# Self-attention scores through one folded weight product

## The reference, cut to what matters

```python
x = x + cross_attention(layernorm(x), ctx)      # 16 heads of 32, context of 257
n = layernorm(x)                                # self-attention, one head of 512
q = n @ Wq + bq;  k = n @ Wk + bk;  v = n @ Wv + bv
scores = einsum('btd,bsd->bts', q, k) / sqrt(512)
scores = where(causal, scores, -1e30)
m = max(scores, axis=(-2, -1));  e = exp(scores - m)
w = e / sum(e, axis=(-2, -1))                   # one sum for a whole 32 x 32 matrix
x = x + einsum('bts,bsd->btd', w, v)
x = x + ffn(layernorm(x))                       # 512 -> 2048 -> 512, signs of the weights
```

## Time and profile before

| | |
|---|---|
| Median of 3 executions | 2920.38 us (2919.47 to 2922.21) |
| Span of the profiled execution | 2917.1 us |
| Median less span | 3.3 us |
| PE busy | 2794.1 us, 96% |
| DVE, ACT, POOL busy | 57%, 43%, 27% |
| Stages in the profile | queries to 126 us, cross-attention to 1918, round 0 to 1997, rounds 1 to 15 and the tail to 2917 |

### The profile page before, as it was taken

How to read it: one execution, slowest core, us unless ns; L and a number is a source line. 1 busy time by engine, 2 the same in 40 slices (tenths; PEclk the granted TensorE clock), 3 DMA queues, 4 the chain that set the end, 5 groups by cost and what they waited for, 6 DMA issues and landing times. The chain is left out here.

```text
span 2917.1 us, 54809 instructions
## 1 busy us (share of the span) xinstructions
PE 2794.1 (96%) x18492; PEld 1704.0 (58%) x18492; DVE 1668.3 (57%) x3620; ACT 1267.4 (43%) x2954; POOL 776.4 (27%) x1530
## 2 busy tenths in 40 slices
PE   7999999999999999999999999957999999899999
PEld 4455555555555555555555555534666666566666
DVE  7555555555555555555555555556665666656664
ACT  4344444444444444444444444423433443344444
POOL 2233333333333333333333333211111111111110
PEclk9999999999999999999999999978999999999999
DMA  4211111111111111111111111022000000000000
GB/s 143 83 56 55 62 41 40 40 48 41 40 40 48 41 40 40 48 41 40 40 48 41 40 40 48 13 84 66 15 30 15 15 14 22 22 14 14 14 23 15
DMA packets 65959, 118.49 MB, mean 41 GB/s; under 512 B 12016, under 2 KB 32496, under 8 KB 65392
## 3 DMA queue, kind: packets, MB, share of 16 engines
q1 hardware_dynamic: 65904, 117.76, 12.4%
HBM read 109.06 MB, written 8.65 MB: 40 GB/s over the span
## 5 line engine op out<-in xcount | busy, mean ns | idle before, releaser
L656 DVE SCALAR_TENSOR_TENSOR kT_lo<-psum,kT_hi 128x512 f16<-128x512 f32 x256 | 177.1, 692 | 440.2 <-ACT kT_hi L587 440.2
L591 ACT ACTIVATE v_hi<-psum 128x512 f16<-128x512 f32 x256 | 152.8, 597 | 552.7 <-PE psum L746 552.7
L746 PE MATMUL psum<-c_hi,xWk_hi 128*128 128x512 f16 x1024 | 388.1, 379 | 2.3 <-PEq L136 2.3
L746 PE MATMUL psum<-xWv_hi,c_hi 128*128 128x512 f16 x1024 | 388.3, 379 | 0.0
L746 PE MATMUL psum<-xWv_lo,c_hi 128*128 128x512 f16 x1024 | 388.1, 379 | 0.0
L746 PE MATMUL psum<-xWv_hi,c_lo 128*128 128x512 f16 x1024 | 388.1, 379 | 0.0
L746 PE MATMUL psum<-c_lo,xWk_hi 128*128 128x512 f16 x1024 | 388.1, 379 | 0.0
L746 PE MATMUL psum<-c_hi,xWk_lo 128*128 128x512 f16 x1024 | 388.1, 379 | 0.0
L118 POOL TENSOR_TENSOR c_lo<-ctx_raw,c_hi 128x1024 f16<-128x1024 f32 x128 | 272.5, 2129 | 429.8 <-ACT c_hi L583 419.2
L662 DVE SCALAR_TENSOR_TENSOR v_lo<-psum,v_hi 128x512 f16<-128x512 f32 x256 | 177.1, 692 | 360.4 <-ACT v_hi L591 360.4
L597 ACT ACTIVATE e<-psum,neg_max 128x257 f32<-128x257 f32 x512 | 236.3, 474 | 281.9 <-DVE neg_max L651 281.9
(11 more groups left out here) (195 smaller groups left out, 5986.9 us busy)
## 6 DMA issues: line engine op xcount, KB each, us to landing
ctx_raw<-in_ctx_main SPq DMA_DIRECT2D x128, 512.0 KB, 3.3
xs<-in_x SPq DMA_DIRECT2D x8, 1024.0 KB, 5.5
v_rep<-v_last_rows SPq DMA_DIRECT2D x512, 16.0 KB, 2.3
xb<-in_x SPq DMA_DIRECT2D x16, 512.0 KB, 3.3
out<-res_out SPq DMA_DIRECT2D x32, 256.0 KB, 2.0
ffn_raw<-in_w_t SPq DMA_DIRECT2D x11, 512.0 KB, 3.4
late_raw<-in_late_w SPq DMA_DIRECT2D x4, 1024.0 KB, 4.7
res<-in_w_t SPq DMA_DIRECT2D x5, 512.0 KB, 3.5
```

The lines of the kernel that those rows point to most:

```text
L591: nc.scalar.mul(v_hi[u][:, t, :], v_bank(t), W_UNSCALE).then_inc(v_hi_done, 1)
L656: nc.vector.scalar_tensor_tensor(out=kT_lo[r][:, m, :, 0:S], in0=k_bank(m), scalar=W_UNSCALE, in1=kT_hi[r][:, m, :, 0:S], op0=ALU.mult, op ...
L746: mm = nc.tensor.matmul(bank, a, b, start=(n == 0), stop=(n == len(steps) - 1))
```

## The change

Since `q k^T = (n Wq + bq)(n Wk + bk)^T`, the scores can be written as `(n F + c) n^T + (n u + d)`, where `F = Wq Wk^T`, `c = Wk bq`, `u = Wq bk` and `d = bq . bk`. The term `n u + d` is one number for each query token, added to its whole row of scores.

In `cross_queries` SP loads bq, bk, Wk and Wq. At the last token group PE transposes both weights (8 times `turn`, 4 float32 transposes each), two ahead of each quarter of the group's projections; then `fold` forms F (48 matmuls of 512 columns), u repeated on all partitions (12 of 512), c (48 of one column) and d (12 of one column). ACT and DVE split the turned weights into the slots of Wo and Wv, which cross-attention fills later, and F into its own. ACT converts the first contexts after the last projection. Two late weights, not four, are loaded in `cross_attention`. In `token_stages` there are two parts r of 24 matmuls, not four, and the scores multiply their result by the transposed tokens themselves. DVE gets `row_biases`: two multiply-and-sum instructions over 128x512 and two additions to the mask. Two DMAs of bias columns at the start of the stage go.

```diff
@@ cross_queries, SP
+            sp.dma_start(bias[:, 0:KC], bq).then_inc(bias_landed, 16)
+            sp.dma_start(bias[:, KC:], bk).then_inc(bias_landed, 16)
+            for u in range(2):
+                load(2 + u, u)
+            load_folded(3)                    # waits for w_lo_done >= 2
+            load_folded(4)                    # waits for w_lo_done >= 3
-            with sp.Fori(1, NG // 2) as i:
+            with sp.Fori(2, NG // 2) as i:
...
@@ cross_queries, PE, last group
                 if not more:
                     last_tokens()
+                    for m in range(KC):
+                        turn(2 * m)
+                        turn(2 * m + 1)
+                        queries(g, u, [m])
+                    fold()
+                    return
+            def turn(j):
...
+                for c in range(KC):
+                    mm = nc.tensor.transpose(psum[:, TURN_BANK[j % 4], c * P:(c + 1) * P],
+                                             raw[1 - j // KC][:, c, k * P:(k + 1) * P], ident[:, :])
+            def fold():
+                pe.wait_ge(turn_lo_done, 2 * KC)
+                for m in range(KC):
+                    accumulate(psum[:, TURN_BANK[m], :],
+                               [(a[:, k, m * P:(m + 1) * P], b[:, k, :]) for k in range(KC)
+                                for a, b in passes(*wqT, *wkT)]).then_inc(fold_ps, 1)
+                pe.wait_ge(rep_done, 2)
+                pe.wait_ge(q_lo_done, NG * KC)
+                accumulate(u_bank, [(a[:, k, :], b[:, k, :]) for k in range(KC)
+                                    for a, b in passes(bk_rep_hi, bk_rep_lo, *wqT)]).then_inc(u_ps, 1)
+                for m in range(KC):
+                    accumulate(c_bank[:, m:m + 1],
+                               [(a[:, k, m * P:(m + 1) * P], b[:, k:k + 1]) for k in range(KC)
+                                for a, b in passes(*wkT, bias_hi, bias_lo)])
+                accumulate(dot_bank, [(a[:, k, :], b[:, k:k + 1]) for k in range(KC)
+                                      for a, b in passes(bk_rep_hi, bk_rep_lo, bias_hi, bias_lo)]
+                           ).then_inc(c_ps, 1)
@@ cross_queries, ACT, last group
                     last_tokens()
+                    for m in range(KC):
+                        high_turned(2 * m)
+                        high_turned(2 * m + 1)
+                        high_q(g, [m])
+                    first_contexts()
+                    for m in range(KC):
+                        high_folded(m)
+                    ...                       # u_row, c_col, bias_dot out of PSUM
@@ token_stages, PE
-                    for r in range(4):
-                        hi, lo = late["sWq" if r < 2 else "sWk"]
+                    for r in range(2):
+                        hi, lo = late["folded"]
...
-                    pe.wait_ge(s["qk_lo_done"], 4 * (n + 1))
+                    pe.wait_ge(s["qk_lo_done"], 2 * (n + 1))
...
-                                                    for q, k in passes(qk_hi, qk_lo, qk_hi, qk_lo)])
+                                                    for q, k in passes(qk_hi, qk_lo, x2T_hi, x2T_lo)])
@@ token_stages, DVE, between the split of x2T and F(5)
+            def row_biases(n):
+                for t in range(T):
+                    dve.wait_ge(s["norm2_done"], T * n + t + 1)
+                    nc.vector.tensor_tensor_reduce(
+                        out=products[:, t, :], in0=xn[:, t, :], in1=u_row[:, :], scale=1.0,
+                        scalar=bias_dot[:, :], op0=ALU.mult, op1=ALU.add,
+                        accum_out=row_bias[:, t:t + 1]).then_inc(s["row_bias_done"], 1)
+                for t in range(T):
+                    dve.wait_ge(s["row_bias_done"], T * n + t + 1)
+                    past(dve, s["sc_done"], BPT * n)
+                    nc.vector.tensor_scalar(row_mask[:, t, :], mask[:, :], row_bias[:, t:t + 1], None,
+                                            ALU.add).then_inc(s["row_mask_done"], 1)
@@ token_stages, SP
-            for dst, src in ((bqk_col[:, 0:KC], bq), (bqk_col[:, KC:], bk), (b1_col[:, :], b1)):
-                sp.dma_start(dst, src).then_inc(s["consts_landed"], 16)
+            sp.dma_start(b1_col[:, :], b1).then_inc(s["consts_landed"], 16)
```

More of the change, by code:

```diff
@@ L21 @@
 FEATURES = 512
+FOLD_SCALE = 16.0
+WO, FOLDED, SWV = range(3)
 def past(engine, semaphore, count):
@@ L56, in perceiver_block @@
     KC = D // P
-    LATE = late_w.shape[0]
+    LATE = 3
     with ExitStack() as whole:
@@ L185, in cross_queries, with turned @@
         v_last_bank = psum[:, 1, :]
+        TURN_BANK = (2, 3, 0, 1)
+        wqT = (late_hi[:, WO], late_lo[:, WO])
+        wkT = (late_hi[:, SWV], late_lo[:, SWV])
+        u_bank = psum[:, 4, :]
+        c_bank = psum[:, 5, 0:KC]
+        dot_bank = psum[:, 5, KC:KC + 1]
+        def turned(j):
+            return (wqT if j < KC else wkT), j % KC
         def t_bank(t):
@@ L291, in low_q, with low_turned @@
                         op1=ALU.subtract).then_inc(q_lo_done, 1)
-            def one(g, u, more=True):
+            def low_turned(j):
+                dve.wait_ge(turn_hi_done, j + 1)
+                (hi, lo), k = turned(j)
+                nc.vector.scalar_tensor_tensor(out=lo[:, k, :], in0=psum[:, TURN_BANK[j % 4], :],
+                                               scalar=W_SCALE, in1=hi[:, k, :], op0=ALU.mult,
+                                               op1=ALU.subtract).then_inc(turn_lo_done, 1)
@@ new lines, in one @@
+            def one(g, u, more=True):
+                if not more:
+                    split_bias()
+                    dve.wait_ge(kl_hi_done, 1)
+                    nc.vector.scalar_tensor_tensor(out=k_last_lo[:, :, :], in0=k_last_bank,
+                                                   scalar=W_UNSCALE, in1=k_last_hi[:, :, :], op0=ALU.mult,
+                                                   op1=ALU.subtract).then_inc(kl_lo_done, 1)
+                    for m in range(KC):
+                        low_turned(2 * m)
+                        low_turned(2 * m + 1)
+                        low_q(g, [m])
+                    for m in range(KC):
+                        low_folded(m)
+                    return
@@ L294, in one @@
                 low_q(g, FIRST)
-                if more:
-                    low_xT(g + 1, 1 - u)
+                low_xT(g + 1, 1 - u)
                 low_q(g, LAST)
@@ L412, in one @@
                     last_tokens()
+                    for m in range(KC):
+                        turn(2 * m)
+                        turn(2 * m + 1)
+                        queries(g, u, [m])
+                    fold()
+                    return
                 queries(g, u, FIRST)
-                if more:
-                    transposes(g + 1, 1 - u)
+                transposes(g + 1, 1 - u)
                 queries(g, u, LAST)
@@ L432, in cross_attention @@
     QUADS = BATCH // 4
-    LATE = late_w.shape[0]
+    LATE = 2
     c_raw, c_hi, c_lo, ctx_landed, c_hi_done, c_lo_done = contexts
@@ L1289, in one @@
                     low_T(s["x2T_hi_done"], x2T_hi, x2T_lo, s["x2T_lo_done"], n)
+                    if isinstance(n, int) and n == 0:
+                        dve.wait_ge(s["mask_done"], BPT)
+                    row_biases(n)
                 F(5)
```

144 lines of the change are left out of this document (109 added, 35 removed).

## The result

| | before | after |
|---|---|---|
| median, us | 2919.93 (2919.16 to 2922.21) | 2847.72 (2846.76 to 2848.47) |
| span of the profiled execution | 2917.1 | 2845.9 |
| cross-attention's first matmul | 126.15 | 147.82 |
| token stage's first matmul | 1920.56 | 1943.83 |
| round 0, from its first token transposes | 60.5 | 55.3 |

The ratio is 0.9751 (0.9737 to 0.9765), 72 us less. The change gave 9 us more than I counted.

What follows compares the result with a forecast made beforehand. PE was taken as the bound in cross-attention and token rounds. Against the span of 2917.1, -78.6 - 4.5 - 0.9 + 19.3 + 0.9 = -63.8 gives 2853.3; with 3.3 for the median, 2856.6, stated as 2857, range 2848 to 2876.

Steps and rivals of the forecast that it cites:

- rounds 1 to 15 and the end: Token stage after its first round: halving the projection matmuls shortens PE's path by 78.6 us in 15 rounds.
- round 0: First token-stage round, paced by DVE with the weight sums: two splits fewer gain 4.5 us, between 0 and 5.2.
- start of the token stage: POOL's wait for the last bias DMA: two DMAs fewer from SP gain 0.9 us, between 0 and 1.
- transposes and fold, fifth load: First stage: new PE work and a later store make it 19.3 us longer; the delayed fifth token load adds 0.9.
- cross-attention: Late weights: splits and two loads leave this stage, where PE is busy at 99.5%, so 0 change.
- median less span: Whole kernel: the median was taken as 3.3 us above the profiled span, before and after the change.
- Projections, rounds 1 to 15: Token-stage projections on PE: half of 96 matmuls at 0.109 us each go, 5.24 us a round, 78.6 in 15.
- store's chain: End of first stage: context conversion, then last value store at 140.7, lets PE start at 145.4, later than PE's own 144.8.
- new wait at the scores: Rival in token-stage rounds: the split or row sums hold the scores, PE loses 18 us, time 2875; chance 0.10.
- dear fold: Rival in the first stage: fold at half clock or costly small matmuls, 9 to 13 us more, 2868; chance 0.10.
- slow sum: Rival in row_biases on DVE: multiply-and-sum below vector rate, at 5.5 us each the time is 2935; chance 0.03.
- bound but PE: Rival in the rounds: removed matmuls were no bound, PE waits later instead, only the fold's cost stays, 2940; chance 0.01.

Runs made afterwards that it cites:

- the two in which the pause is short and the clock steady: The changed kernel and the kernel before, each with DVE's low half of gelu 2 moved ahead of the second normalisation: 2805.78 and 2864.61 us.
- the two other pairs of kernels: Kernels before and after with DVE's gelu 2 part moved (2864.61, 2805.78 us); with POOL held back too (2837.79, 2772.43, the last also with store and load reordered).

## Why the prediction was nearly right, and what failed

| step | forecast, us | measured | by |
|---|---|---|---|
| rounds 1 to 15 and the end | -78.6 | -89.5 | periods |
| round 0 | -4.5 | -5.2 | 60.5 to 55.3 |
| start of the token stage | -0.9 | +0.2 | 15.95 to 16.12 from first matmul to transposes |
| transposes and fold, fifth load | +19.3 + 0.9 | +21.7 | 126.15 to 147.82 |
| cross-attention | 0 | +1.6 | 1794.4 to 1796.0 |
| sum, against the span | -63.8 | -71.2 | |
| median less span | 3.3 | 1.8 | |

**The step that failed** is in "Projections, rounds 1 to 15": half of 10.48 us go, "5.24 us a round, 78.6 us in 15". The 5.24 holds. What was wrong is what I did not write: that all the rest of the round keeps its length. The time that a round loses at the lower clock was in my sum at no change, without a reason. I had a sign of it in hand. In the round that I read, 60.02 us long at a clock of 0.95, the first matmul after the pause took 0.59 and the transposes 1.91; I used that only to price a rival in the first stage, and never asked what the same clock does in a shorter round. The clock gave 10.9 us more, and that is the error: with these the forecast would have been 2846. That the loss falls from 2.17 to 1.20 because the round holds 48 matmuls less is shown by the kernels in which they are put back, and that it hangs on the pause by the two in which the pause is short and the clock steady. Why the clock falls after one 3.58 us pause and not after the next is open, and no row of the trace of before gives 1.20. The error left a trace in the range as well: its low end was made of terms at nothing and had no row for the clock, which could move either way.

A second term was mis-sized: the median less the span, 3.3. I had taken a median of three executions less the span of another, faster one. In every execution on record that has both, the time lies 1.7 to 1.9 us above its own span, and 1.8 is what came; that is 1.5 us of the 9.

**What held.** The matmuls were on the path one for one. The scores have no wait in the round read, with the 1.2 us left that I worked out. The sums are at vector rate, 0.744 where I took 0.75, and lie in DVE's idle time. The Trainium skill's rule that an instruction with an accumulator and two sources that are not bf16 runs at half rate (Vector Engine (DVE) Microarchitecture Reference, "Points that are easy to get wrong") did not apply here: 0.744 us against 0.69 for a plain two-operand pass. The trace names the sum a custom instruction with a read of the accumulator of its own, so whether the page means this form is not shown. Nor would it have changed the time. The wait at F(4) is the same to the tenth. The store's chain, not PE, ends the first stage, as forecast.

**Terms that were off by a little.** The 60 one-column matmuls took 1.5 us (from 141.85 to 143.34, 0.025 each) and not 3.4; since the store's chain ended last, this gave nothing. The Trainium skill (TensorE: Matmul & The Clock Gate, "Wait — 56ns, not 53.3ns?") says that starts come no closer than about 25 ns however few columns there are; these agree. The same page's "LDWEIGHTS (loading the stationary operand)" gives 107 ns for a load of 128 columns. The loads' rows last 0.10 us each here, which agrees, but they too start 0.025 apart: they overlap, so the 6.4 us that I had worked out from that figure as a price of the 60 did not come. The fifth load came 2.66 us later to DVE (62.70 against 60.04) and PE was 1.7 late (its values start at 112.46 and not at 110.76), where I took 0.9. From the store to the next stage it took 1.0 longer. Cross-attention took 1.6 longer. It begins with eight matmuls at the lower clock, 0.43 apart instead of 0.22, which would make 1.7; but the kernel with the load behind the tokens begins with seven such and takes 1794.1, and the stage varies from there to 1797.4 among kernels that share its code, so this cause is not shown. Two DMAs fewer gave nothing at the token stage's start: POOL waits 9.30 us for the bias row and waited 9.13, so that wait did not hang on the two issues. Round 0 gave 5.2, the upper end of my bounds; that is in part luck, since it gave 2.9 and 3.6 in the two other pairs of kernels (60.35 to 57.45 and 60.13 to 56.55). Together these, without the clock in the rounds, come to 3.5 us against me on the span. The sum closes: -10.9 of the rounds, +3.5 and -1.5 of the median less the span are the -8.9 between 2856.6 and 2847.7.

**The rivals.** None of the four came about: no new wait at the scores (1.30 us in round 0, 1.25 before), no dear fold (PE's own part took 18.0 us, 143.4 less 123.7 and the 1.7 by which it began late, where I took 19.9), no slow sum, and no bound but PE.

## What to carry to other kernels

Matmuls that PE runs without a gap behind are worth their start-to-start time, and this can be worked out from the trace to about a hundredth of a microsecond; but only where the clock is steady. Where a round has a pause of PE of some microseconds, look at the periods of many rounds and not at one: equal work with different lengths, and a granted clock under 1.00, say that each round carries a loss that any change of its length may move, both ways, so give the range a term of that loss's size. Then look for what makes the pause: here one part moved in DVE's queue, which cost nothing, gave 42 us after the change and 55 before it.

## What was not expected of the hardware

After the same pause of 3.58 us the clock fell in some rounds and not in others, with no order that the records explain: 8 of 13 rounds after, all 13 of them before. Twelve added matmuls cost 1.87 us a round where the next twelve cost 0.76. One-column matmuls start 25 ns apart. And two 128x512 normalisations on DVE take 1.00 us alone and 2.42 beside POOL's copies. The clock fell in cross-attention after a pause of only 0.57 us that followed 60 one-column matmuls.
